# Router and rank-16 products of a vision tower with 98 tokens as the stationary operand

## The reference, cut to what matters

```python
h = h + _L0_ffn_ref(_layernorm(h, axis=-1), ...)

def _L0_ffn_ref(x, ...):                       # x: 64 x 196 tokens x 256
    base_out = einsum('bsi,oi->bso', x, base_W) + base_b
    shared_out = einsum('bsr,or->bso', einsum('bsi,ri->bsr', x, shared_A), shared_B)
    logits = einsum('bsi,ei->bse', x, router_W) + router_b      # 6 experts
    gate = softmax(logits)
    sparse_w = the two largest of gate, the others 0, divided by their sum + 1e-6
    h = einsum('bsi,eri->bser', x, routed_A)                    # 6 x 16 = 96 columns
    routed_out = einsum('bseo,bse->bso', einsum('bser,eor->bseo', h, routed_B), sparse_w)
    return base_out + shared_out + routed_out
```

## Time and profile before

| what | value |
|---|---|
| time, median of 3 runs | 1343.94 us (1343.25 to 1344.47) |
| span of the profiled execution, first to last instruction | 1346.5 us |
| mean granted TensorE clock over the span | 0.981 |
| PE busy | 1310.8 us, 97% |
| VectorE busy | 943.2 us, 70% |
| ScalarE busy | 644.0 us, 48% |
| GpSimd busy | 283.0 us, 21% |

### The profile page before, as it was taken

One profiled execution on the slowest core, in us unless ns is written; L12 is line 12 of the kernel. 1 busy time (PEld: TensorE's weight loads), 2 busy tenths in 40 slices (PEclk: granted clock), 3 DMA queues, 4 the chain that ended last, 5 costly groups with the idle time before them and its releaser, 6 DMA issues.

```text
span 1346.5 us, 23512 instructions
## 1 busy us (share of the span) xinstructions
PE 1310.8 (97%) x8008; PEld 1273.8 (95%) x8008; DVE 943.2 (70%) x2571; ACT 644.0 (48%) x1169; POOL 283.0 (21%) x395
## 2 busy tenths in 40 slices
PE   6899999999999999999999999999999999999986
PEld 6889999999999999999999999999999999999975
DVE  5467776677676677676677676767776667767675
ACT  4544554444554444555444555444455444455421
POOL 3322221211221211221221222120222121222000
PEclk8899999999999999999999999999999999999986
DMA  7011101111100111110111110111110111110000
GB/s 237 1 36 49 49 12 37 48 48 48 48 24 23 48 48 48 48 39 10 48 48 48 48 48 0 48 48 48 48 48 3 45 48 48 48 49 13 1 12 25
DMA packets 18203, 56.40 MB, mean 42 GB/s; under 512 B 2160, under 2 KB 13528, under 8 KB 14168
## 3 DMA queue, kind: packets, MB, share of 16 engines
q1 hardware_dynamic: 17320, 54.93, 11.8%
q10 hardware_dynamic: 816, 0.79, 0.2%
HBM read 42.87 MB, written 12.85 MB: 41 GB/s over the span
## 4 chain that ended last, share of the span: by engine, by line
PE 95%; DVE 2%; ACT 1%; issue 1%; POOL 1%; DMA 0%; POOLq 0%; DVEq 0%
PE big L954 25%; PE big L955 24%; PE big L956 24%; PE turn L1061 4%; PE turn L987 4%; PE turn L994 3%; PE turn L1045 2%; PE turn L955 1%; PE turn L954 1%; PE turn L956 1%; PE gate_ps L954 1%; PE gate_ps L1035 1%; PE gate_ps L955 1%; PE gate_ps L956 1%; PE gate_ps L1068 1%
## 5 line engine op out<-in xcount | busy, mean ns | idle before, releaser
L347 POOL TENSOR_TENSOR patches_l<-patches,patches_h 128x392 fp32r<-128x392 f32 x186 | 189.2, 1046 | 928.6 <-ACT patches_h L421 928.6
L467 ACT ACTIVATE gelu<-big,biases 128x392 f32<-128x392 f32 x256 | 149.2, 584 | 112.6 <-PE big L956 111.4
L954 PE MATMUL big<-gelu_h,w_h 128*128 128x392 f32 x512 | 180.9, 353 | 0.0
L954 PE MATMUL big<-x_h,w_h 128*128 128x392 f32 x512 | 178.1, 348 | 1.4 <-ACT gelu L467 1.4
L440 ACT ACTIVATE norm<-turn,ln_tmp 98x256 f32<-98x256 f32 x128 | 62.1, 565 | 243.3 <-DVE ln_tmp L689 243.3
L955 PE MATMUL big<-gelu_l,w_h 128*128 128x392 f32 x512 | 175.5, 343 | 0.0
L956 PE MATMUL big<-gelu_h,w_l 128*128 128x392 f32 x512 | 174.5, 341 | 0.0
L955 PE MATMUL big<-x_l,w_h 128*128 128x392 f32 x512 | 174.2, 340 | 0.0
L956 PE MATMUL big<-x_h,w_l 128*128 128x392 f32 x512 | 174.2, 340 | 0.0
L954 PE MATMUL big<-patches_h,tokw_h 128*128 128x392 f32 x384 | 136.9, 356 | 10.0 <-POOL patches_l L359 7.6
L955 PE MATMUL big<-patches_l,tokw_h 128*128 128x392 f32 x384 | 133.4, 347 | 0.0
(11 more groups left out here) (154 smaller groups left out, 2828.0 us busy)
## 6 DMA issues: line engine op xcount, KB each, us to landing
patches<-dram_xg SPq DMA_DIRECT2D x31, 1176.0 KB, 5.5
out<-result SPq DMA_DIRECT2D x32, 392.0 KB, 2.7
patches<-dram_xg SPq DMA_DIRECT2D x3, 392.0 KB, 5.0
prod<-dram_tok_w ACTq DMA_DIRECT2D x3, 256.0 KB, 6.8
gelu<-dram_w SPq DMA_DIRECT2D x1, 512.0 KB, 7.3
h_sb<-dram_w SPq DMA_DIRECT2D x1, 512.0 KB, 8.4
result<-dram_w SPq DMA_DIRECT2D x1, 384.0 KB, 6.3
x_proj<-dram_in_w SPq DMA_DIRECT2D x1, 256.0 KB, 6.7
```

The source lines that it names most:

```text
L347: pool.tensor_tensor(patches_l[:, k, :], patches[:, k, :], patches_h[:, k, :].bitcast(F32), ALU.subtract).then_inc(pool_patches_lo, 1)
L467: act.activation(gelu[:, k % 4, :], big[UP_BANK[k]][:, 0:GT], ACT.Gelu, bias=b1_bias[:, k:k + 1]).then_inc(act_gelu, 1)
L954: pe.matmul(ps, w_h, x_h, start=first, stop=False)
```

## The change

`route` swaps the operands of its products: 98 tokens of x2 are stationary, the 102 columns of `route_w` are moving, once for each of four tiles, and the result lands with tokens on partitions, where VectorE reads it. The eviction on ScalarE, `turn_route` and their two semaphores are gone. The router's bias is now a broadcast constant of 98 x 24 that VectorE adds as the first operation of `gate_exp`, through a new slot of `gate_wide`; it costs one more constant transfer at the start (`CONSTS` 10), and the bias column leaves `biases`. `GATE_STEPS` and `EXP_STEPS`, the counts of a semaphore, grow by one.

```diff
@@ start, SyncE
             const(rank_thr[:, :], rank_thr_d)
+            const(router_bias[:, :], router_bias_d)
@@ ScalarE
-            def route(g):
-                act.wait_ge(pe_route, g + 1)
-                act.activation(route_sb[:, :], gate_ps[0:ROUTE_COLS, 0:GT], ACT.Identity,
-                               bias=route_bias).then_inc(act_route, 1)
...
@@ VectorE, gate_exp
-                logits = rows[:, :, ROUTED:ROUTE_COLS]
-                dve.wait_ge(pe_turn_route, g + 1)
+                logits = gate_wide[:, 11]
+                dve.wait_ge(pe_route, g + 1)
+                link(dve.tensor_tensor(logits, rows[:, :, ROUTED:ROUTE_COLS],
+                                       router_bias[:, :].rearrange("p (t e) -> p t e", t=TILES), ALU.add))
                 link(dve.tensor_reduce(small(0), logits, AX_X, ALU.max))
@@ PE
             def route(g):
-                for c in range(DH):
-                    pe.wait_ge(dve_x2_lo, DH * g + c + 1)
-                    ins = mm3(gate_ps[0:ROUTE_COLS, 0:GT], route_h[:, c, :], route_l[:, c, :], x2_h[:, c, :],
-                              x2_l[:, c, :], c == 0, c == DH - 1)
+                pe.wait_ge(dve_x2_lo, DH * g + DH)
+                for t in range(TILES):
+                    toks = slice(t * TT, (t + 1) * TT)
+                    for c in range(DH):
+                        ins = mm3(gate_ps[0:TT, t * ROUTE_COLS:(t + 1) * ROUTE_COLS], x2_h[:, c, toks],
+                                  x2_l[:, c, toks], route_h[:, c, :], route_l[:, c, :], c == 0, c == DH - 1)
                 ins.then_inc(pe_route, 1)
-
-            def turn_route(g):
-                pe.wait_ge(act_route, g + 1)
-                for t in range(TILES):
-                    ins = pe.transpose(gate_ps[0:TT, t * ROUTE_COLS:(t + 1) * ROUTE_COLS],
-                                       route_sb[:, t * TT:(t + 1) * TT], ident[0:ROUTE_COLS, 0:ROUTE_COLS])
-                ins.then_inc(pe_turn_route, 1)
```

More of the change, by code:

```diff
@@ L63 @@
 BANK = 512
-CONSTS = 9
+CONSTS = 10
 CHUNK = 2
@@ L78 @@
 LN_STEPS = 16
-GATE_STEPS = 24
-EXP_STEPS = 13
+GATE_STEPS = 25
+EXP_STEPS = 14
 def exists(g):
@@ L90, in tower_program @@
                   shared_a, shared_bt, route_w, routed_bt, biases_d, ident_d, cos_fwd_d, sin_fwd_d, cos_inv_d,
-                  sin_inv_d, cos_tap_d, sin_tap_d, rank_thr_d, out):
+                  sin_inv_d, cos_tap_d, sin_tap_d, rank_thr_d, router_bias_d, out):
     ctx = ExitStack()
@@ L116, in tower_program @@
         rank_thr = sb("rank_thr", [TT, TILES * EXPERTS * EXPERTS])
-        biases = sb("biases", [P, 4 * DH + HC + 1])
+        router_bias = sb("router_bias", [TT, TILES * EXPERTS])
+        biases = sb("biases", [P, 4 * DH + HC])
         in_bias = biases[:, 0:DH]
@@ L122, in tower_program @@
         b1_bias = biases[:, 4 * DH:4 * DH + HC]
-        route_bias = biases[0:ROUTE_COLS, 4 * DH + HC:4 * DH + HC + 1]
         patches = sb("patches", [P, KT, GT])
@@ L143, in tower_program @@
         y_h, y_l = pair("y", [P, DH, GT])
-        route_sb = sb("route_sb", [ROUTE_COLS, GT])
         gated = sb("gated", [TT, TILES, ROUTED])
@@ L156, in tower_program @@
         gate_small = sb("gate_small", [TT, 8, TILES])
-        gate_wide = sb("gate_wide", [TT, 11, TILES, EXPERTS])
+        gate_wide = sb("gate_wide", [TT, 12, TILES, EXPERTS])
         gate_cmp = sb("gate_cmp", [TT, 2, TILES, EXPERTS, EXPERTS])
@@ L204, in tower_program @@
         pe_route = sem("pe_route")
-        pe_turn_route = sem("pe_turn_route")
         pe_turn_gated = sem("pe_turn_gated")
@@ L220, in tower_program @@
         act_x2_hi = sem("act_x2_hi")
-        act_route = sem("act_route")
         act_gated_hi = sem("act_gated_hi")
@@ L509, in step @@
                     project(mid)
-                if exists(tail):
-                    route(tail)
                 if exists(mid):
@@ L597, in drain @@
                 x2_hi(back)
-                route(back)
                 gated_hi(back)
@@ L1113, in first_half @@
                     mlp_up(mid, 0)
-                if exists(tail):
-                    turn_route(tail)
                 if exists(back):
@@ L1240, in drain @@
                 route(back)
-                turn_route(back)
                 for m in range(DH):
@@ L1297 @@
                ("attn_in_b", "attn_mod_b2", "attn_out_b", "ffn_base_b", "attn_mod_b1")]
-    route_column = np.zeros((1, P), np.float32)
-    route_column[0, ROUTED:ROUTE_COLS] = a[pre + "ffn_router_b"]
-    biases = np.concatenate([*columns, route_column]).T
+    biases = np.concatenate(columns).T
+    router_bias = np.broadcast_to(a[pre + "ffn_router_b"], (TT, TILES, EXPERTS)).reshape(TT, -1)
     arrays = {
@@ L1315 @@
         **consts,
+        "router_bias": router_bias,
     }
```

## The result

The changed kernel takes 1379.45 us (median of 4 runs, 1379.18 to 1381.59) against 1343.6 us of the kernel before in the same series (4 runs, 1343.01 to 1344.47): ratio 1.0267, interval 1.0254 to 1.0279. It is slower by 35.9 us where 22.0 were forecast, and the time lies 3.5 us above the upper end of the range. The sign was right and so was the price of a product; a cost of about 13 us is missing from the sum.

What follows compares the result with a forecast made beforehand. PE's own instruction stream was taken as the bound: 30 steady groups at +0.71 us (+21.3) and +0.7 for group 31 gave +22.0 us on 1343.94, so 1365.9 us was forecast, range 1341 to 1376.

Steps and rivals of the forecast that it cites:

- PE is the bound, and the sign: Whole kernel: PE, busy 97%, sets the time; slower by over 0.2% was given a chance of 0.91.
- The distance p: New `route`: time between starts of neighbouring narrow products, taken as 0.088 us, from 0.084 to 0.099.
- rival (a): New `route`: weight loads limit the products, 0.084 to 0.099 us apart, giving 1363 to 1374.5 us; chance 0.76.
- (b) to (d): New `route`: streaming decides, 1335 us, 0.05; loads hide in part, 1341 to 1347, 0.04; no overlap, 1401, 0.04.
- (e): New `route`: narrow float32r products cost what plain float32 does, 48 records for 24 products, 1436 us; chance 0.11.
- +0.71 a steady group: Steady steps, groups 0 to 29: 24 new products cost 2.11 us in place of 1.40, together +21.3 us.
- Group 30 nothing: Drain: group 30's longer route costs nothing, since PE then waits for VectorE's spectrum anyway.
- group 31 +0.7: Drain: group 31's exposed route at a granted clock of 0.50 takes about 4.6 us against 3.91, +0.7 us.
- The edits costed at nothing: Removed ScalarE eviction, VectorE bias add, wait for both x2 halves and extra constant transfer: no time change, being covered.
- The sum: Whole kernel: +21.3 for groups 0 to 29 and +0.7 for group 31 make +22.0 us, giving 1365.9 us.
- The signs of being wrong: Listed profile signs: other product distances or 48 records, PE waiting for gated or folded data, steady granted clock leaving 1.00.
- no new waits of PE: Sign of being right: PE stays near 97% busy and its profile shows no added waits.

Runs made afterwards that it cites:

- e6: e1 plus one VectorE memset of `gate_ps`, with 52 of 102 moving columns in the route products: 1374.4 us, ratio 1.0222.
- e7: e1 plus one VectorE memset of `gate_ps`, with 49 of 98 stationary columns in the route products: 1347.39 us, ratio 1.0027.
- e1: The changed kernel with PE's loop over the steps written out, its instructions in the steps unchanged: 1366.39 us, ratio 1.0163.
- e5: The kernel before with PE's loop written out: 1343.52 us, ratio 0.9995.
- e2: The changed kernel, loop kept, with 130 PE instructions that only raise an unused semaphore ahead of PE's first wait: 1380.37 us, ratio 1.0263.
- e8: The changed kernel, loop kept, moved by 100 PE instructions (25 small unread products where PE waits anyway in step 0): 1366.85 us, ratio 1.0172.
- e3: The kernel before with 84 semaphore-only PE instructions ahead of PE's first wait: 1350.68 us, ratio 1.005.
- e4: The kernel before with 40 semaphore-only PE instructions ahead of PE's first wait: 1350.26 us over 10 runs (1347.17 to 1365.98), ratio 1.007.

## Why the prediction was right or wrong

- **PE is the bound, and the sign.** Right: PE stays at 97%, and the kernel is slower by a multiple of what a measurement can tell.
- **The distance p.** Right: 0.088 was taken, 0.087 is measured, and the loads last 167 ns where 162 were forecast. e6 and e7 settle what the slope of the load durations had suggested: rival (a) holds. (b) to (d) fall by the distance itself, and (e) because the 24 products are 24 records; 0.050 comes only with half the columns to load.
- **+0.71 a steady group.** Right, 2.29 against 1.58 us. With the loop's cost taken out on both sides (e1 less e5) the change costs 22.9 us where the sum has 22.0.
- **Group 30 nothing, group 31 +0.7.** Right for 30 (4.07 us from route to inverse transform against 4.11). For 31 it is +0.58, the products 0.167 apart at a granted clock of 0.50, where 0.168 was taken.
- **The edits costed at nothing.** Right: the bias addition has 2.98 us of idle time ahead of it, PE got no new wait for VectorE or ScalarE, and no gain from ScalarE's missing 0.59 us a group shows beside the price of the products. One row was read loosely: the 0.47 us of the earlier trace rows stand ahead of the eviction itself; ahead of the next GELU tile (667.96) ScalarE idled 0.57 us, which gives the same cover.
- **The sum.** Here it failed. "A change is worth what it adds to or takes from that stream" was read as the time of the added products, so the sum went straight from 30 x 0.71 + 0.7 to the result. That the 448 products are also instructions, 84 more in each turn of PE's loop, has no term, no rival and no place in the range. The signs of being wrong name waits for data and a lower clock, not a wait for code; what failed to hold was the sign "no new waits of PE", by eight waits. e1, e2 (less what its filler costs) and e8 show the missing term, three ways to take it away: 13.1, 12.3 and 12.6 us. Added to the sum it gives 22.0 + 13.1 = 35.1 of the 35.9 measured.
- **What could have been seen.** The kernel before showed 16 packets on its instruction queue for the whole program and none while its loop turned, so it turned without a fetch. That, the sizes given by the page of the Trainium skill quoted with the experiments, and a count of the instructions in a turn would have made "the longer loop no longer turns for nothing" a rival. A chance could be given, not a certainty: the number of instructions ahead of the loop that the runtime adds isn't in the profile, and e3 and e4 show how much hangs on it.
- **The base.** The profiled run of before had a slower beginning: its first route started at 103.8 us, that of the changed kernel at 99.9. The spans (1346.5 and 1377.3) are therefore 30.8 apart and the times 35.9. Anchoring the forecast on the median of the runs avoided that error; comparing the spans would have hidden 5 us of the miss.

No version tried beats the kernel before. The best form of the change is e1 or e8, 1.6 to 1.7% slower than it. Keeping the wide product and turning only the six logit rows was not tried.

## What to carry to other kernels

Swapping the operands so that a result lands already transposed costs loads: with this type a loaded column takes 0.087/98 = 0.89 ns and a streamed one some 0.44 (from the rows of 392 and 512 columns), so by that estimate a product should stream about twice as many columns as it loads, and here 24 pairs of 98 and 102 cost 2.09 us where six wide products and four transposes cost 1.40. When an edit changes how many instructions a hardware loop holds, read the packets of the instruction queue and the waits of the kind "issue" at its turns before and after, and run it once with the loop written out: 13 of these 36 us had nothing to do with the work. An experiment that adds an instruction needs a control that adds the same instruction and nothing else; 8 us came here from a single one.

## What the hardware showed that was not expected

- A turn of PE's loop whose code had to come again cost 1.53 us, and nine packets of 16 KB arrived for each; the same loop 100 or 130 instructions further on turned for nothing.
- An empty operation of PE that raises a semaphore took 0.16 us (130 in 20.8, 84 in 13.8 us).
- One VectorE instruction ahead of all its steps, on PSUM or on SBUF alike, cost 7.6 to 7.8 us over the kernel, as 0.37 us ahead of one and the same instruction in two steps of three. Why isn't settled.
- With the loop of the kernel before moved by 40 instructions (e4), two turns of eight fetched their code again, nine packets each, and the time was not steady: ten runs spread over 19 us, which is near the 21 us estimated for eight such turns.
